# Slot offsets of the first layer's software pipeline in a two-layer decoder kernel

## The chip, the cores and the metric

The kernel runs on one core of one Trainium2 chip. The metric is the device time of one execution in microseconds (us). Five engines work side by side: PE (TensorE, matrix products; its weight loads are PEld), DVE (VectorE), ACT (ScalarE), POOL (GpSimd) and SP (SyncE, which here only issues DMAs). Each has its own instruction stream, executed in the order in which it was written. They are tied together by semaphores alone.

## The reference, cut to what matters

The program is a decoder of two layers. Each has a self-attention, a cross-attention against a context and a feed-forward part, each followed by a residual sum and a layer norm. The change touches the attentions of the first layer only. Per batch element (16 of them, 128 positions of 256 channels) they compute:

```
q, k, v = bitlinear(x, w_q), bitlinear(x, w_k), bitlinear(x, w_v)   # rows rounded to 8 bits, ternary weights
a = softmax(q k^T / 4, causal) v            # 16 heads; the sequence is seen as 256 tokens of 256
x1 = layernorm(x + bitlinear(a, w_o))
q = rope(wq x1 + bq); k = rope(wk c + bk); v = wv c + bv
x2 = layernorm(x1 + wo softmax(q k^T / sqrt(8), mask) v + bo)       # 16 heads of 8 channels
```

x2 goes to DRAM (`x_mid`), and its logits for the choice of experts are kept. Routing, the experts, the second layer and the retrieval part follow; the change does not touch them.

## The kernel before

`first_layer_attentions` (L529) is a software pipeline over the 16 batch elements. Time is cut into numbered slots. `Slots(20)` (L491) says that a new batch element starts every 20 slots: a step with offset `o` is written for batch element `b` into slot `20 b + o`. Each engine's program is one loop over the slots. In each slot it holds, in a fixed order, the steps whose offset fits. A slot is no barrier. It only sets the order of the instructions within each engine's stream, and an engine goes on as soon as its semaphores let it. I call `offset mod 20` the place of a step: in the steady part of the pipeline all steps with the same place stand in the same slot, for different batch elements. So offset -25 and offset 95 both have place 15.

Two lanes of small pieces fill the slots (`Lane`, L508). The **query lane** computes scores with queries as rows: 4 own (self-attention) pieces and 16 cross pieces per batch element. Of each, DVE takes the row maxima straight from the PSUM bank (`reduce_maxima`, L443, rows L447 and L449). There are two such banks, so PE may write piece i only when DVE has reduced piece i-2 (`pe.wait_ge(reduced, i - 1)`, L695). The maxima are split in two bf16 parts (`own_two`, `cross_two`), turned by PE (L379), copied by ACT and laid by DMA as two more rows into the operand stack (`own_rows`, `cross_rows`, `lay_maxima` L345, DMA rows L350 and L352). The **key lane** then computes the scores again with keys as rows and the maxima subtracted by those rows; ACT takes their exponential (L892), and every fourth piece PE weighs the values with them (`own_values`, `cross_values`, L422 and L438). Both lanes hold 20 pieces in 20 slots, so each has a piece in every slot of the steady part.

The other steps of a batch element, by engine:

- DVE: `row_scales_of` (L473 to L480 and L1032), `round_rows_of` (L486, L488), `copy_v` (L1043), `own_heads` (L1072, L1074), `head_scales`, `round_heads`, `own_sum` with its moments (L1088, L464 to L468), `own_end` (L1095), `rotate` (L1101, L1102; for q and for k), `cross_recips` (L1109), `cross_heads` (L1113), `cross_sum` with its moments (L1117), `cross_end` (L1125), `keep_logits`. In a slot the reduction of the query piece comes first, then these.
- POOL: `root` (L1011), and `split_self` and `split_cross` (L336 to L342), which split an operand into three bf16 parts.
- SP: loads of x (L610) and of the context (L615), the DMAs that lay the parts into the stacks (`stack_part` L355, `stack_side` L367), the store of x2 (L631). SP waits in order: what is written behind a waiting DMA waits too.
- PE: the small products and transposes between these. They share the PSUM bank `work` (query, key and value products), the bank `bank_a` (own values, heads, output product) and a small bank (maxima, sums, output, logits), and wait on the semaphores of whoever read the bank last. `make_cross_v` (L792), for one, waits until DVE has rotated k (`k_rotated`).

DMA rows are named by their issuing queue: SPq, ACTq.

Of the kernel before, what the change touches and what calls it, by code (L numbers as in the profile page):

```python
# [528 lines left out]
def first_layer_attentions(nc, d, t, ps):  # L529

    ctx = ExitStack()
    with ctx:
# [53 lines left out]
        block = ctx.enter_context(nc.Block())  # L586

        slots = Slots(20)
        OWN_SCORES, CROSS_SCORES, OWN_KEYS, CROSS_KEYS = 0, ((39, 1), (44, 15)), 9, ((65, 4), (73, 12))
        LOAD_ROWS, ROW_SCALES, ROUND_ROWS, TURN_ROWS, COPY_ROWS, MAKE_QK, SCALE_QK, MAKE_V, COPY_V, TURN_QK, COPY_QK = -33, -25, -24, -18, -18, -16, -16, -14, -13, -12, -12  # L590
        SPLIT_SELF, STACK_FIRST, STACK_SECOND, STACK_THIRD = -8, -7, -6, -5
        OWN_TWO, TURN_OWN_MAXIMA, OWN_ROWS, OWN_VALUES, COPY_OUT, TURN_OUT, OWN_HEADS, HEAD_SCALES, ROUND_HEADS = 3, 5, 5, 14, 15, 17, 18, 19, 20
        TURN_HEADS, COPY_HEADS, MAKE_O, OWN_SUM, ROOT_A, OWN_END = 22, 22, 24, 25, 25, 27
        LOAD_CONTEXT, MAKE_CROSS_K, ROTATE_K, SPLIT_KEYS, STACK_KEYS = 5, 11, 12, 15, 25
        MAKE_CROSS_Q, ROTATE_Q, SPLIT_QUERIES, STACK_QUERIES = 29, 29, 30, 31
        MAKE_CROSS_V, COPY_CROSS_V, CROSS_TWO, TURN_CROSS_MAXIMA, CROSS_ROWS = 53, 53, 58, 60, 60
        CROSS_VALUES = (70, 78, 82, 86)
        COPY_CROSS_OUT, CROSS_RECIPS, LAY_RECIPS, SPREAD_SUMS, CROSS_HEADS, MAKE_Y, CROSS_SUM, ROOT_X, CROSS_END = 87, 89, 90, 92, 92, 94, 95, 96, 98
        STORE_ROWS, TURN_X2, COPY_X2, MAKE_LOGITS, KEEP_LOGITS = 99, 101, 101, 103, 104
        query_lane = slots.lane(OWN_SCORES, CROSS_SCORES, SELF0.banks, CROSS0.banks)  # L600
        key_lane = slots.lane(OWN_KEYS, CROSS_KEYS, SELF0.banks, CROSS0.banks)
        SLOTS = range(LOAD_ROWS, slots.window * (B - 1) + KEEP_LOGITS + 1)
# [51 lines left out]
        def _(pe):  # L654
# [140 lines left out]
            def cross_values(b, g):  # L795
                i = key_lane.index("cross", b, GROUP * g)
                if g == 0:
                    pe.wait_ge(xv_copied, 2 * b + 2)
                    if b >= 1:
                        pe.wait_ge(out_x_copied, b)  # L800
                pe.wait_ge(probs_made, i + GROUP)
                weigh_shared(pe, out_x, [probs[(i + j) % RING] for j in range(GROUP)], t["v_cross0"][b % 2], GROUP * g).then_inc(probs_used, 1)
# [31 lines left out]
            for s in SLOTS:  # L834
# [16 lines left out]
                for g in range(4):  # L851
                    if (b := slots.batch_at(s, CROSS_VALUES[g])) is not None:
                        cross_values(b, g)
# [685 lines left out]
def second_layer_attentions(nc, d, t, ps):  # L1539

    ctx = ExitStack()
    with ctx:
# [140 lines left out]
        def _(pe):  # L1683
# [85 lines left out]
            def own_values(b):  # L1769
                i = key_lane.index("own", b, 0)  # L1770
                if b >= 1:
                    pe.wait_ge(sum_a_made, b)
                pe.wait_ge(v_copied, b + 1)
                pe.wait_ge(probs_made, i + GROUP)
                weigh_values(pe, SELF1, bank_a, [probs[(i + n) % RING] for n in range(GROUP)], t["v_self1"][b % 3], 0).then_inc(probs_used, 1)
# [19 lines left out]
            def cross_values(b, n):  # L1795
                i = key_lane.index("cross", b, n)
                if n == 0 and b >= 1:
                    pe.wait_ge(sum_x_made, b)
                if n == 0:
                    pe.wait_ge(xv_copied, b + 1)  # L1800
                pe.wait_ge(probs_made, i + GROUP)
                weigh_values(pe, CROSS1, out_x, [probs[(i + j) % RING] for j in range(GROUP)], t["v_cross1"][b % 2], n).then_inc(probs_used, 1)
# [27 lines left out]
            for s in SLOTS:  # L1830
# [14 lines left out]
                if (b := slots.batch_at(s, OWN_VALUES)) is not None:  # L1845
                    own_values(b)
                if (b := slots.batch_at(s, CROSS_VALUES)) is not None:
                    cross_values(b, 0)
# [723 lines left out]
def program(nc, d, out):  # L2572

    ctx = ExitStack()
    with ctx:
# [25 lines left out]
        with ExitStack() as stage:  # L2601
            sb, _ = open_tensors(nc, stage, "kept")
            for att, n in ((SELF0, 2), (CROSS0, 3)):
                t[f"stack_{att.name}"] = [sb(f"stack_{att.name}_{u}", [att.rows + 2] + ([att.groups, 2 * D] if att.causal else [2, att.groups, D]), BF16) for u in range(n)]
            t["v_self0"] = [sb(f"v_self0_{u}", [P, HEADS, 32]) for u in range(2)]
            t["v_cross0"] = [sb(f"v_cross0_{u}", [P, 2 * XG // SHARED, 2, GROUP, 32]) for u in range(2)]
            prepare_weights(nc, d, t, ps)
            first_layer_attentions(nc, d, t, ps)
# [39 lines left out]
```

## Time and profile before

| | us |
|---|---|
| median of 3 runs | 1780.8 |
| lowest, highest run | 1767.7, 1783.01 |
| the profiled execution | 1767.65 |
| its span in the trace | 1765.9 |
| PE busy, share of the span | 1422.5, 81% |
| DVE busy | 975.9, 55% |
| ACT busy | 614.0, 35% |
| POOL busy | 418.3, 24% |

```profile
PE   2466888888888986399999993568888875899997
DVE  5456666666666652522222223367878752567775
PEclk9878999999999998599999996789999997899999
```

Each digit is the busy share of one fortieth of the span (44.1 us) in tenths; PEclk is the clock that TensorE was granted, in tenths of 2.4 GHz. The first layer's attentions lie in slices 2 to 16: their first score product starts at 60.60 us, the last logits are kept at about 711 us. Busy times are not a bound by themselves: what matters is which wait ends last in each stretch.

### The profile page before, as it was taken

Reading aid. Unit: us, or ns where it says so; the run is one execution under the profiler, and the core shown is the slowest. Engines: PE = TensorE matmul, PEld = TensorE weight load, DVE = VectorE, ACT = ScalarE, POOL = GpSimd, SP = SyncE. Lnnn points to the kernel's source line nnn. Section 1 sums busy time; section 2 is a strip of 40 time slices with the busy share of each in tenths; the row PEclk is TensorE's granted clock in tenths of the full one; section 3 lists DMA queues with packets and bytes.
Section 4 is the critical chain, followed back from the end, with each engine's and each line's share of the span. In section 5 each row is a group of like instructions: output and inputs, shape, how many; then the busy total and the mean of one; then the engine's idle time right before and its main releaser. Section 6 shows DMA issues by size and latency. Waiting matters only on the chain. (4 is left out here: it accounts for less than half of the span.)

```text
span 1765.9 us, 29494 instructions
## 1 busy us (share of the span) xinstructions
PE 1422.5 (81%) x9331; PEld 878.0 (50%) x9331; DVE 975.9 (55%) x2623; ACT 614.0 (35%) x1389; POOL 418.3 (24%) x588
## 2 busy tenths in 40 slices
PE   2466888888888986399999993568888875899997
PEld 1234555555555553155656562345555543566554
DVE  5456666666666652522222223367878752567775
ACT  0122444434444443022222231335555542232231
POOL 2233223322223200111111103454555420000000
PEclk9878999999999998599999996789999997899999
DMA  3245344533444310651111102664555420200000
GB/s 89 58 50 66 47 60 53 64 51 54 54 53 56 45 24 9 233 180 68 32 35 34 33 25 55 172 119 103 113 110 118 98 51 20 72 1 13 12 1 25
DMA packets 165337, 112.77 MB, mean 64 GB/s; under 512 B 32690, under 2 KB 155826, under 8 KB 165056
## 3 DMA queue, kind: packets, MB, share of 16 engines
q1 hardware_dynamic: 150272, 99.04, 27.7%
q0 software_dynamic: 3408, 9.31, 2.2%
q10 hardware_dynamic: 11504, 2.53, 0.8%
q8 instruction: 78, 1.28, 0.3%
q14 instruction: 75, 0.61, 0.1%
HBM read 46.48 MB, written 12.45 MB: 33 GB/s over the span
## 5 line engine op out<-in xcount | busy, mean ns | idle before, releaser
L892 ACT ACTIVATE first_probs<-pair 128x512 f32<-128x512 f32 x320 | 190.3, 597 | 302.6 <-PE pair L408 273.4
L449 DVE TENSOR_REDUCE first_negmax_x<-bank 128x2 f32<-128x512 f32 x256 | 177.0, 692 | 109.5 <-PE bank L393 96.1
L1885 ACT ACTIVATE second_probs<-pair 128x512 f32<-128x512 f32 x192 | 113.8, 598 | 129.2 <-PE pair L408 112.6
L393 PE MATMUL bank<-kept_stack_cross 96*128 96x256 bf16 x768 | 150.4, 277 | 9.7 <-DMA kept_stack_cross<-second_parts_x_q 7.9
L408 PE MATMUL pair<-kept_stack_cross 98*128 98x256 bf16 x768 | 148.8, 276 | 1.5 <-DMA kept_stack_cross<-second_rows_x 1.0
L1439 PE MATMUL pair<-kept_w,experts_hidden_t 128*128 x312 | 141.5, 596 | 0.0
L386 PE MATMUL bank<-kept_mask_q,kept_ident 128*128 128x512 bf16 x256 | 99.3, 388 | 35.0 <-DVE first_negmax_x L449 26.8
L449 DVE TENSOR_REDUCE second_negmax_x<-bank 128x2 f32<-128x512 f32 x128 | 88.5, 692 | 60.2 <-PE bank L393 52.2
L393 PEld LDWEIGHTS bank<-kept_stack_cross 96*128 96x128 bf16 x768 | 74.1, 101 | 74.3 <-issue 21.2
L1480 ACT ACTIVATE experts_hidden_t<-bank,kept_b 128x128 f32<-128x128 f32 x156 | 44.4, 367 | 187.4 <-PE bank L1414 187.4
L1394 POOL DMA_INDIRECT experts_expert_rows<-x_mid,kept_row_of x39 | 36.9, 947 | 276.4 <-PE bank L1406 250.3
L401 PE MATMUL pair<-kept_mask_t,kept_ident 128*128 128x512 bf16 x256 | 98.4, 384 | 2.5 <-ACT first_probs L892 1.5
L1439 PEld LDWEIGHTS pair<-kept_w,experts_hidden_t 128*128 128x128 f32 x312 | 60.0, 193 | 76.0 <-issue 76.0
L408 PEld LDWEIGHTS pair<-kept_stack_cross 98*128 98x128 bf16 x768 | 74.5, 100 | 41.5 <-issue 3.5
L386 PE MATMUL bank<-kept_causal_q,kept_ident 128*128 128x512 bf16 x128 | 53.5, 418 | 48.9 <-DMA kept_stack_self<-first_parts_a 24.6
L1517 DVE COPY experts_hidden<-pair 128x512 f32<-128x512 f32 x39 | 27.0, 691 | 108.7 <-PE pair L1439 108.7
L1430 PE MATMUL bank<-kept_w,experts_expert_rows_t 128*128 x156 | 77.9, 624 | 5.5 <-DMA kept_w<-in_L_ffn_W 4.1
L1448 PE MATMUL pair<-kept_w,experts_hidden_t 128*128 x312 | 73.9, 380 | 1.4 <-ACT experts_hidden_t L1488 1.4
L438 PE MATMUL pair<-first_probs,kept_v_cross 128*32 128x256 f32 x1024 | 68.5, 385 | 3.7 <-ACT first_probs L892 3.7
L401 PE MATMUL pair<-kept_causal_t,kept_ident 128*128 128x512 bf16 x128 | 53.0, 414 | 20.0 <-DMA kept_stack_self<-first_rows_a 19.2
L2442 POOL TENSOR_TENSOR retrieve_stats<-retrieve_stats,kept_minus_half 128x1 f32<-128x1 f32 x16 | 8.9, 557 | 251.3 <-DVE retrieve_stats L468 251.3
L1511 DVE COPY experts_hidden<-bank 128x512 f32<-128x512 f32 x39 | 27.0, 691 | 71.2 <-PE bank L1430 71.2
(430 smaller groups left out, 2974.1 us busy)
## 6 DMA issues: line engine op xcount, KB each, us to landing
kept_stack_self<-first_parts_a SPq DMA_DIRECT2D x128, 64.0 KB, 5.6
kept_w<-in_L_ffn_W SPq DMA_DIRECT2D x16, 512.0 KB, 7.5
kept_w<-in_L_ffn_W SPq DMA_DIRECT2D x8, 1024.0 KB, 7.0
kept_stack_self<-second_parts_a SPq DMA_DIRECT2D x128, 64.0 KB, 3.4
kept_stack_cross<-first_parts_x_k SPq DMA_DIRECT2D x96, 64.0 KB
kept_stack_cross<-first_parts_x_q SPq DMA_DIRECT2D x96, 64.0 KB
kept_stack_cross<-second_parts_x_k SPq DMA_DIRECT2D x96, 64.0 KB
kept_stack_cross<-second_parts_x_q SPq DMA_DIRECT2D x96, 64.0 KB
```

The lines of the kernel that those rows point to most:

```text
L386: pe.matmul(bank[:, :], ident16, mask, start=True, stop=False, skip_group_check=True)
L393: mm = pe.matmul(out, q, k, start=mask is None, stop=True, skip_group_check=True)
L401: pe.matmul(bank[:, :], ident16, mask, start=True, stop=False, skip_group_check=True)
L408: mm = pe.matmul(out, k, q, start=mask is None, stop=True, skip_group_check=True)
L438: mm = pe.matmul(out[j * 32:(j + 1) * 32, at * D:(at + 1) * D], values[:, 2 * k + at, a, j, :], probs[j][:, k * D:(k + 1) * D], start=(a = ...
L449: return dve.tensor_reduce(negmax[:, 2 * n:2 * n + 2], bank[:, :].rearrange("p (m t) -> p m t", t=D), AX.X, ALU.max, negate=True)
L892: act.activation(probs[i % RING][:, :], key_bank[i % 2][:, :], ACT.Exp, scale=att.scale).then_inc(probs_made, 1)
L1430: mm = pe.matmul(layer1_bank[:, :], rows_t[n % 2][:, k, :], t["w1"][:, bass.ds(expert, 1), k, :].rearrange("p a f -> p (a f)"), start=(k = ...
L1439: mm = pe.matmul(layer2_bank[:, :], hidden1_t[n % 2][:, k, :], t["w2"][:, bass.ds(expert, 1), k, :].rearrange("p a f -> p (a f)"), start=( ...
L1448: mm = pe.matmul(layer3_bank[:, 0:D], hidden2_t[n % 2][:, k, :], t["w3"][:, bass.ds(expert, 1), k, :].rearrange("p a f -> p (a f)"), start ...
L1480: ins = act.activation(hidden1_t[n % 2][:, k, :], turn1_bank[:, k * P:(k + 1) * P], ACT.Gelu, bias=t["b12"][:, k, bass.ds(expert, 1)])
L1885: act.activation(probs[i % RING][:, :], key_bank[i % 2][:, :], ACT.Exp, scale=att.scale).then_inc(probs_made, 1)
```

## The change

Only numbers move. No instruction is added or taken away, and the order inside a slot is the same. The last slot of the loop is 410 instead of 404, its first one -31 instead of -33.

```
-        OWN_SCORES, CROSS_SCORES, OWN_KEYS, CROSS_KEYS = 0, ((39, 1), (44, 15)), 9, ((65, 4), (73, 12))
-        LOAD_ROWS, ROW_SCALES, ROUND_ROWS, TURN_ROWS, COPY_ROWS, MAKE_QK, SCALE_QK, MAKE_V, COPY_V, TURN_QK, COPY_QK = -33, -25, -24, -18, -18, -16, -16, -14, -13, -12, -12
-        SPLIT_SELF, STACK_FIRST, STACK_SECOND, STACK_THIRD = -8, -7, -6, -5
-        OWN_TWO, TURN_OWN_MAXIMA, OWN_ROWS, OWN_VALUES, COPY_OUT, TURN_OUT, OWN_HEADS, HEAD_SCALES, ROUND_HEADS = 3, 5, 5, 14, 15, 17, 18, 19, 20
-        TURN_HEADS, COPY_HEADS, MAKE_O, OWN_SUM, ROOT_A, OWN_END = 22, 22, 24, 25, 25, 27
-        LOAD_CONTEXT, MAKE_CROSS_K, ROTATE_K, SPLIT_KEYS, STACK_KEYS = 5, 11, 12, 15, 25
-        MAKE_CROSS_Q, ROTATE_Q, SPLIT_QUERIES, STACK_QUERIES = 29, 29, 30, 31
-        MAKE_CROSS_V, COPY_CROSS_V, CROSS_TWO, TURN_CROSS_MAXIMA, CROSS_ROWS = 53, 53, 58, 60, 60
-        CROSS_VALUES = (70, 78, 82, 86)
-        COPY_CROSS_OUT, CROSS_RECIPS, LAY_RECIPS, SPREAD_SUMS, CROSS_HEADS, MAKE_Y, CROSS_SUM, ROOT_X, CROSS_END = 87, 89, 90, 92, 92, 94, 95, 96, 98
-        STORE_ROWS, TURN_X2, COPY_X2, MAKE_LOGITS, KEEP_LOGITS = 99, 101, 101, 103, 104
+        OWN_SCORES, CROSS_SCORES, OWN_KEYS, CROSS_KEYS = 0, ((44, 16),), 11, ((67, 4), (75, 12))
+        LOAD_ROWS, ROW_SCALES, ROUND_ROWS, TURN_ROWS, COPY_ROWS, MAKE_QK, SCALE_QK, MAKE_V, COPY_V, TURN_QK, COPY_QK = -31, -26, -24, -18, -18, -16, -16, -14, -13, -12, -12
+        SPLIT_SELF, STACK_FIRST, STACK_SECOND, STACK_THIRD = -10, -9, -8, -7
+        OWN_TWO, TURN_OWN_MAXIMA, OWN_ROWS, OWN_VALUES, COPY_OUT, TURN_OUT, OWN_HEADS, HEAD_SCALES, ROUND_HEADS = 3, 5, 5, 16, 17, 19, 21, 23, 24
+        TURN_HEADS, COPY_HEADS, MAKE_O, OWN_SUM, ROOT_A, OWN_END = 26, 26, 28, 29, 29, 31
+        LOAD_CONTEXT, MAKE_CROSS_K, ROTATE_K, SPLIT_KEYS, STACK_KEYS = 5, 14, 15, 16, 27
+        MAKE_CROSS_Q, ROTATE_Q, SPLIT_QUERIES, STACK_QUERIES = 33, 33, 34, 36
+        MAKE_CROSS_V, COPY_CROSS_V, CROSS_TWO, TURN_CROSS_MAXIMA, CROSS_ROWS = 57, 57, 59, 61, 61
+        CROSS_VALUES = (72, 80, 84, 88)
+        COPY_CROSS_OUT, CROSS_RECIPS, LAY_RECIPS, SPREAD_SUMS, CROSS_HEADS, MAKE_Y, CROSS_SUM, ROOT_X, CROSS_END = 89, 92, 93, 96, 97, 99, 100, 101, 105
+        STORE_ROWS, TURN_X2, COPY_X2, MAKE_LOGITS, KEEP_LOGITS = 106, 107, 107, 109, 110
```

A pair `(r, m)` of a lane stands for m pieces in slots r, r+1, and so on. Before, the first cross score of a batch element stood alone in slot 39, ahead of the next element's own scores. Now all 16 stand in slots 44 to 59.

## Rows read from the trace of the kernel before

**Rows 1.** Part 1 of the page: busy time of each engine, share, instructions

```profile
PE 1422.5 (81%) x9331; PEld 878.0 (50%) x9331; DVE 975.9 (55%) x2623; ACT 614.0 (35%) x1389; POOL 418.3 (24%) x588
```

**Rows 2.** Stretches: length, busy us per engine, granted clock, DMA share, GB/s

```profile
211.50:582.00 370.50, 315.52 (x2762) 194.92 (x2760) 244.47 (x596) 158.04 (x320) 111.24 (x160) 0.99 0.42 56
320.50:357.10 36.60, 31.12 (x279) 19.26 (x278) 24.40 (x61) 15.81 (x32) 11.13 (x16) 1.00 0.45 57
582.00:664.50 82.50, 72.42 (x602) 42.90 (x600) 52.41 (x114) 35.18 (x70) 11.97 (x20) 1.00 0.19 29
```

**Rows 3.** PE's waits, 211.5 to 582: total us, times, longest

```profile
PE bank L386 <- DVE first_negmax_x L449: 22.1, 20, 1.8
PE pair L401 <- DMA kept_stack_self<-first_rows_a: 14.1, 9, 1.7
PE bank L386 <- DVE first_negmax_a L447: 9.1, 10, 1.4
PE bank L792 <- issue: 7.4, 10, 0.7
```

**Rows 4.** Timeline 349.8 to 354.5: start, us, engine, line, operation, idle before

```profile
349.83 0.69 DVE L449 TENSOR_REDUCE first_negmax_x<-bank 128x2 f32<-128x512 f32 x1 [2.25 <-PE bank L393]
...
350.07 0.38 PE L386 MATMUL bank<-kept_mask_q,kept_ident 128*128 128x512 bf16 x1
...
350.44 0.48 DVE L1117 SCALAR_TENSOR_TENSOR first_sum_x<-pair,kept_bo,first_x 128x256 f32<-128x256 f32 x1
...
350.95 0.38 PE L386 MATMUL bank<-kept_mask_q,kept_ident 128*128 128x512 bf16 x1
...
351.88 0.42 DVE L473 TENSOR_REDUCE first_qs<-first_x 128x1 f32<-128x256 f32 x1
...
353.45 0.69 DVE L449 TENSOR_REDUCE first_negmax_x<-bank 128x2 f32<-128x512 f32 x1
354.06 0.34 DVE L486 TENSOR_SCALAR first_whole<-first_x,first_qs 128x256 f32<-128x256 f32 x1
...
354.20 0.39 PE L386 MATMUL bank<-kept_mask_q,kept_ident 128*128 128x512 bf16 x1 [1.77 <-DVE first_negmax_x L449]
```

**Rows 5.** Timeline 365 to 374: the maxima's rows and what waits for them

```profile
365.37 3.97 SPq L374 DMA_DIRECT2D kept_stack_cross<-first_parts_x_k  x6
...
367.73 1.33 ACTq L350 DMA_DIRECT2D kept_stack_self<-first_rows_a  x2
...
373.85 0.39 PE L401 MATMUL pair<-kept_causal_t,kept_ident 128*128 128x512 bf16 x1 [1.70 <-DMA kept_stack_self<-first_rows_a]
```

**Rows 6.** Timeline 383 to 385: the rotation of k and the value product

```profile
383.67 0.47 DVE L1102 SCALAR_TENSOR_TENSOR first_sind_k<-bank,kept_bqk_rot,kept_sin 128x256 f32<-128x256 f32 x1
...
384.25 0.68 PE L792 MATMUL bank<-kept_xw_t,first_kv 128*128 128x128 f32 x4 [0.74 <-issue]
```

**Rows 7.** A stretch of 3.4 us at the lower clock

```profile
374.30:377.70 3.40, 3.40 (x14) 2.18 (x12) 1.59 (x4) 0.60 (x1) 0.32 (x1) 0.50 0.00 0
```

**Rows 8.** PE's waits for stacked operands, 60.6 to 211.5

```profile
PE bank L386 <- DMA kept_stack_self<-first_parts_a: 24.6, 5, 10.6
PE bank L386 <- DMA kept_stack_cross<-first_parts_x_q: 8.1, 2, 6.7
```

**Rows 9.** Timeline 89 to 110: from the third element's operands to its scores

```profile
89.11 0.60 ACT L912 ACTIVATE first_full_a<-bank 128x512 f32<-128x512 f32 x1 [3.48 <-PE bank L685]
...
93.98 3.90 SPq L374 DMA_DIRECT2D kept_stack_cross<-first_parts_x_q  x6
...
96.09 1.05 POOL L336 TENSOR_TENSOR first_parts_a<-first_full_a,kept_ones_bf 128x512 bf16<-128x512 f32 x1
...
96.34 0.95 DVE L486 TENSOR_SCALAR first_whole<-first_x,first_qs 128x256 f32<-128x256 f32 x1
...
103.77 1.23 SPq L362 DMA_DIRECT2D kept_stack_self<-first_parts_a  x1
...
109.77 0.61 PE L386 MATMUL bank<-kept_causal_q,kept_ident 128*128 128x512 bf16 x1 [4.73 <-DMA kept_stack_self<-first_parts_a]
```

## The prediction

> **What bounds the kernel now.** I read the busy shares first. PE is busy 81% of the span, DVE 55% [rows 1], so the whole leans on PE, but the share says nothing of the stage that changes. So I cut the first layer into stretches. Between 211.5 and 582 us the pipeline is full: ten batch elements take 370.5 us, and PE is busy for 315.5 of them. One undisturbed element takes 36.6 us with 31.1 of PE work; DVE's is 24.4 and POOL's 11.1 [rows 2]. So about 5.4 us per element are PE idle. PE's work stays, and the question is only how much of that idle time the new places remove.
>
> PE's waits in the same stretch name it [rows 3]. DVE's maxima come late for 22.1 + 9.1 = 31.2 us, the DMA with the own maxima for 14.1, and the value product L792 stands 7.4 us with "issue" as its releaser. They make 52.7 us of the 55.0 that are idle.
>
> **Change, part 1: DVE's pile-up at places 15 and 16.** Before, place 15 holds the reduction, the cross sum with its moments and the row scales; place 16 adds the rounding. The timeline shows it [rows 4]: reduction at 349.83, cross sum at 350.44, row scales at 351.88, and the next reduction only at 353.45, that is 3.6 us for one slot of DVE. PE passes a bare slot in 350.95 - 350.07 = 0.88 us, fills both score banks and waits 1.77 us. This is the largest of the waits. After the change the cross sum has place 0, the row scales 14, the rounding 16. I lay out the whole window of 20 slots with the rows' prices: reduction 0.7 plus 0.6 from the start of a score piece until it can be reduced, a sum with moments 1.45 and row or head scales 1.5 [rows 4], a rotation 0.95 from two instructions of 0.47 [rows 6], 0.88 for PE's two pieces, and the rest of PE's 31.1 us laid on the slots where its steps now stand. The fullest slot of DVE becomes place 3 (reduction, own maxima, head scales: 2.6 us), and place 4 has 1.5 us of extra PE work to cover it. Two tight spots are left. At places 9 to 12 PE has two nearly bare slots, while DVE has the own sum: the piece of place 12 waits about 0.6 us. At places 13 and 14 the key product now follows the query product by one slot, and the bank is free only when DVE has rotated q: about 0.25 us. With small ones elsewhere that makes 1.1 us per element. The bounds are 0 (all is covered) and the present 3.1 per element. I take 1.5, nearer to the layout because its prices are rows of this trace, a little above it because it has no jitter.
>
> **Part 2: L792.** The value product needs k rotated. DVE ends that at 384.14 and PE starts at 384.25 [rows 6], so "issue" hides a wait on DVE, one slot behind the rotation. Now the rotation has place 15, the product 17, and behind the second stands 2 us of other PE work at place 16. The 7.4 us go; what could remain is inside the 1.5 above.
>
> **Part 3: own keys two slots later.** The maxima's rows are issued by ACT from 367.73 to 369.06 and released PE at 373.85 after 1.70 us of waiting [rows 5]. Transit is 4.8 us, behind six DMAs of SP (365.37 to 369.34) on the same engines. The turning stays at place 5, the keys go from 9 to 11. Places 9 and 10 are 1.25 and 0.88 us of PE, and values that used to be weighed at other places now fall on place 8. So PE arrives at least 2.1 us later, against 1.7 that it was late. The 14.1 us go. If they went on being late by their difference it would be a few tenths; if the transit doubled, all of it would stay. SP's six key DMAs move from place 5 to 7, so they start slightly behind the rows instead of ahead; that helps rather than hurts.
>
> Sum for the steady stretch: 52.7 removed, 15 put back, so **-38**.
>
> **Part 4: the clock.** At 374.30, right behind that wait, TensorE's clock falls from 2.4 to 1.2 GHz for 3.4 us [rows 7], and PE is busy all through it, so it costs about half, 1.7 us. The stretch's mean is 0.99 [rows 2], 1% of 370.5 us off full speed, which is 3.7 us of the lower level's half and so about three such falls. Where PE does not wait, they have no cause that I can see. I take **-4**; between 0 and -5. The Trainium skill says the same (TensorE: Matmul & The Clock Gate, Part 1: activity releases the throttle); by it all three would go.
>
> **Part 5: filling the pipeline.** Up to 211.5 us PE waits for stacked operands, 24.6 and 8.1 us [rows 8]. The first wait, 10.6 us, is the first element's latency and stays. For the third element see the timeline [rows 9]: its operands are ready at 89.7, but POOL splits them only at 96.09, since the first element's query split stands before it, and SP has six query DMAs in front (93.98 to 97.88). The last part is issued at 103.77 and PE starts at 109.77. Now the own split (place 10) stands ahead of the query split (14). It starts near 90.5, because the root at place 9 still precedes it; SP needs about 6.5 us for its ten DMAs, then 6 us of transit: near 104, 6 us earlier. Besides the 10.6 and the 4.7 at 109.77, 9.3 us of such waits are left; I lay nearly all on the two elements that follow, for the same reason. Against this, cross scores start 5 slots later for the first element. I take **-15**, between -5 (half of each wait comes back as another) and -21.
>
> **Part 6: draining.** From 582 to 664.5 PE is idle for 10.1 of 82.5 us [rows 2]; of this I count 5 as the same waits. But more work is left behind slot 300: one score piece, two key pieces and about a fifth of the other steps of one element, 3 us. Net **-2**, between +3 and -5. The last chain of the stage, value sums to logits, keeps its steps, and an empty slot costs nothing.
>
> What moves without a price: the load of x (place 7 to 9) stands 5 slots ahead of its use instead of 8; rival C. The store of x2 and the logits move by 6 to 7 slots, nothing waits for them inside the stage. The reciprocals get 3 slots after the copy, not 2. The x1, key-stack and probability buffers keep their distances.
>
> **Sum.** -38 - 4 - 15 - 2 = -59. The profiled execution took 1767.65, so its like takes 1708.6. The median shown is 13 us above that execution, the lowest run equals it; I add half of the distance and predict **1714 us**.
>
> **A rule that speaks against it.** The split on POOL now runs beside other DVE steps. While POOL works on L336 (96.09 to 97.14), DVE's L486 takes 0.95 us [rows 9] instead of 0.34 [rows 4]. The Trainium skill says why (SBUF, State Buffer, "Who interferes with whom"): DVE and GpSimd share a pair of ports, and one holds it for a whole instruction. In the new order `own_end` at place 11 falls beside the own split and the rounding at 16 beside the key split. Three instructions held by 0.6 to 1 us each make up to 2.2 us of DVE per element. In the layout DVE runs ahead at both places, so I price it at nothing; without that cover it is rival B.
>
> **The rivals.**
> A. DVE's waits do not go, they move: places 9 to 15 hold the own sum, both rotations and the row scales. For: these are 5 of DVE's longest steps within 7 slots, and PE's slots there are short. Against: none shares a slot with another. Then 31.2 + 7.4 stay and the steady part brings 14: -14 - 15 - 2 = -31, 1743 with the same half distance.
> B. The shared ports: 2.2 us for each of some 14 elements give back 31 of 59: -28, 1746. For: the row at 96.34. Against: DVE is idle for a third of the element [rows 2].
> C. **Slower**: SP's queue. The load of x has place 9, and it waits for the own sum of three elements earlier, which now has place 9 as well. It is issued some 2 us into place 9 and the row scales need it about 9.4 us into it. Transit is at most the 6 us of the stacks, so there is 1 us of slack. It decides from a transit of 13 us on: then DVE stands 4.5 us per element, all that parts 1 to 3 bring; at 16 us it would cost 3 us times 14, +25 on balance, 1799. Against: SP's other DMAs at that time are few.
> D. No change worth measuring: the saved waits come back as waits on operands, as PE reaches each DMA's landing sooner. 1774.
>
> **Chances.** Forecast 0.70, A 0.12, B 0.06, D 0.07, C 0.05. A measurement of this kernel can tell about 1% (18 us) from no change. Faster by over 1%: forecast, A and B, 0.88; within 1%: D, 0.07; slower: C, 0.05. The range starts at 1690, where nearly all idle time and all of part 5 go (-80 on the lowest run), and goes up to 1750, which takes in A and B. Left out are D, C and the tails of the forecast, 0.2 in all.
>
> **What would show it.** Right: elements in the full stretch take 32 to 33 us instead of 36.6; DVE's waits before L386 fall below 1.5 us per element; no wait of L401 on the own rows; L792 without its 0.74; own scores of the third element near 104 us; PEclk 1.00 from about 180 to 560 us. Wrong: a wait of DVE's L473 for x (C), L1095 or L486 near 1 us together with waits of PE (B), or PE's waits gathered before the pieces of places 12 to 15 (A).

## The result, and the profile after

The changed kernel takes 1688.6 us (median of 4 runs, 1686.03 to 1690.56) where the kernel before took 1774.25 in the same comparison: a ratio of 0.9515, 95% interval 0.9482 to 0.9549. That is 86 us less. I forecast 60 less, with 1690 as the lower end, so the direction was right and the size too small. The profiled execution took 1686.03, its span is 1684.2; 81.7 us of span are gone.

Parts 1 and 2 of the page after (busy time; tenths in 40 slices of 42.1 us):

```profile
PE 1400.9 (83%) x9221; PEld 874.6 (52%) x9331; DVE 982.0 (58%) x2623; ACT 609.2 (36%) x1389; POOL 419.8 (25%) x588
...
PE   2478999999999954899999946588888875999997
...
PEclk9679999999999976999999976799999996999999
```

Counted from 1, PE is at 9 in slices 5 to 14, where it stood at 8 in all but one. This trace lacks 110 of PE's 9331 matmul records (x9221), so its PE busy times are a little low and the idle rows of PE are bounds.

Stretches of both kernels, cut where the 1st, 3rd, 6th and 16th element's own scores begin, then at the end of the scores and of the stage (columns: stretch, length, busy of PE, PEld, DVE, ACT, POOL, clock, DMA share, GB/s). After:

```profile
60.50:99.70 39.20, 24.77 (x188) 15.33 (x190) 19.28 (x51) 10.54 (x21) 16.00 (x22) 0.76 0.30 63
99.70:188.60 88.90, 75.14 (x605) 47.69 (x617) 68.09 (x157) 32.15 (x67) 33.48 (x48) 0.89 0.42 68
188.60:505.10 316.50, 302.24 (x2712) 191.69 (x2761) 248.42 (x593) 152.60 (x320) 112.16 (x160) 1.00 0.38 65
505.10:583.60 78.50, 72.84 (x612) 43.48 (x623) 53.90 (x117) 34.62 (x70) 11.94 (x20) 1.00 0.22 31
583.60:626.80 43.20, 28.72 (x216) 14.83 (x217) 8.63 (x25) 15.81 (x31) 1.65 (x3) 0.85 0.04 12
626.80:1684.20 1057.40, 884.71 (x4837) 553.98 (x4868) 554.25 (x1568) 360.33 (x876) 228.69 (x320) 0.92 0.28 72
```

And the same of before, where [rows 2] do not hold it:

```profile
60.60:109.80 49.20, 26.52 (x194) 16.21 (x195) 21.90 (x60) 10.18 (x21) 17.60 (x24) 0.77 0.42 62
109.80:211.30 101.50, 80.30 (x637) 49.17 (x638) 66.68 (x152) 32.69 (x68) 32.29 (x46) 0.89 0.47 54
...
664.50:710.50 46.00, 30.84 (x215) 15.27 (x215) 8.02 (x22) 15.25 (x29) 1.09 (x2) 0.80 0.04 11
710.50:1765.90 1055.40, 882.88 (x4868) 551.23 (x4868) 552.59 (x1568) 359.55 (x876) 228.20 (x320) 0.92 0.28 72
```

Filling (to the 6th element's scores) went from 150.7 to 128.1 us, -22.6. The full stretch of ten elements went from 370.6 to 316.5, -54.1, so an element now takes 31.65. Draining went from 128.6 to 121.7, -6.9. All that follows: +2.0. The gain lies where it was forecast (-38 and -4 in the full stretch, -15 in filling, -2 in draining), and each stretch gained more than its terms.

The changed kernel was profiled once more in a later comparison (a0_changed). That trace has all 9331 matmul records, so its idle time of PE in the full stretch can be trusted: 316.90 - 306.04 = 10.9 us, where it was 55.0 before.

```profile
188.40:505.30 316.90, 306.04 (x2762) 191.80 (x2761) 248.12 (x593) 152.61 (x320) 111.97 (x160) 1.00 0.38 65
```

PE's waits in the full stretch, which answer to [rows 3]:

```profile
PE bank L386 <- DVE first_negmax_x L449: 4.4, 12, 0.4
PE bank L773 <- issue: 3.7, 6, 0.9
...
PE bank L386 <- DVE first_negmax_a L447: 0.5, 1, 0.5
```

31.2 us for DVE's maxima have become 4.9. L401's wait for the rows and L792's for the rotation are gone. The key product L773 waits now, as the layout by hand had it for places 13 and 14: 0.37 us per element, where it had 0.25. The waits named by these rows are 8.6 us (9.0 in a0_changed) where I had put back 15.

The third element's operands, timeline after, to be read beside [rows 9]:

```profile
88.59 0.60 ACT L912 ACTIVATE first_full_a<-bank 128x512 f32<-128x512 f32 x1 [1.87 <-PE bank L685]
...
89.54 1.05 POOL L336 TENSOR_TENSOR first_parts_a<-first_full_a,kept_ones_bf 128x512 bf16<-128x512 f32 x1
...
97.35 0.60 SPq L362 DMA_DIRECT2D kept_stack_self<-first_parts_a  x1
...
99.75 0.10 PEld L386 LDWEIGHTS bank<-kept_causal_q,kept_ident 128*128 128x128 bf16 x1 [3.22 <-DMA kept_stack_self<-first_parts_a]
...
100.15 0.63 PE L393 MATMUL bank<-kept_stack_self 96*128 96x128 bf16 x4 [3.39 <-DMA kept_stack_self<-first_parts_a]
```

The split starts 6.6 us earlier and the last part is issued 6.4 us earlier. PE goes on at 99.75, where the weights for the first own score are loaded (the record of its product is one of those missing). That is 2.4 us after the last issue, not 6.0: the transit fell to less than half as well. In a0_changed, whose records are complete, it is 2.5.

### The profile page after: what moved, and what is told of

The parts are those of the page before. It is cut to its first block and busy times, and to the rows that moved or that the text cites. A ratio compares the mean times of both kernels' runs of the same rounds, so it can differ in the third digit from the quotient of the medians.

```text
span 1684.2 us, 29387 instructions
## 1 busy us (share of the span) xinstructions
PE 1400.9 (83%) x9221; PEld 874.6 (52%) x9331; DVE 982.0 (58%) x2623; ACT 609.2 (36%) x1389; POOL 419.8 (25%) x588
## 5 line engine op out<-in xcount | busy, mean ns | idle before, releaser
L1885 ACT ACTIVATE second_probs<-pair 128x512 f32<-128x512 f32 x192 | 113.7, 598 | 130.8 <-PE pair L408 111.6
L1480 ACT ACTIVATE experts_hidden_t<-bank,kept_b 128x128 f32<-128x128 f32 x156 | 44.6, 368 | 186.4 <-PE bank L1414 186.4
L386 PE MATMUL bank<-kept_mask_q,kept_ident 128*128 128x512 bf16 x221 | 86.4, 391 | 20.4 <-DVE first_negmax_x L449 11.8
L401 PE MATMUL pair<-kept_mask_t,kept_ident 128*128 128x512 bf16 x249 | 94.7, 380 | 1.8 <-ACT first_probs L892 1.8
L1488 ACT ACTIVATE experts_hidden_t<-bank,kept_b 128x128 f32<-128x128 f32 x156 | 44.7, 368 | 50.3 <-PE bank L1422 50.3
L2315 PE MATMUL pair<-retrieve_x_t,kept_gate_w 128*128 128x512 f32 x128 | 61.9, 607 | 0.0
```

The source lines that it names most:

```text
L386: pe.matmul(bank[:, :], ident16, mask, start=True, stop=False, skip_group_check=True)
L401: pe.matmul(bank[:, :], ident16, mask, start=True, stop=False, skip_group_check=True)
L1885: act.activation(probs[i % RING][:, :], key_bank[i % 2][:, :], ACT.Exp, scale=att.scale).then_inc(probs_made, 1)
L2315: mm = pe.matmul(bank[:, :], t[weights][:, j, u * P:(u + 1) * P], x5_t[g % 2][:, j, :], start=(j == 0), stop=(j == KT - 1))
```

## The experiments

Offsets of the same code, changed in the kernel before (b...) or in the changed one (a..., c...). The table has the time, its ratio to the kernel before in the same comparison, and from one profile of each the filling, the full stretch (ten elements) and the draining. The draining ends here with the last logits, a few tenths of a us before the ends taken above. An effect on the time is told against the kernel that the run started from: the one before in the same comparison for b..., a0_changed (1687.2) for a... and c1_key_product, which were timed in other comparisons than a0_changed.

| kernel | median us | ratio, 95% interval | filling | full | draining |
|---|---|---|---|---|---|
| before | 1773 to 1776 | 1 | 150.7 | 370.6 | 128.0 |
| b1_scales | 1756.95 | 0.9905 (0.9878 to 0.9931) | 150.9 | 356.1 | 128.0 |
| b2_value | 1762.97 | 0.9935 (0.9907 to 0.9963) | 150.0 | 362.8 | 127.7 |
| b3_keys | 1832.47 | 1.0326 (1.0281 to 1.0372) | 162.2 | 412.3 | 134.1 |
| b4_split | 1768.14 | 0.9952 (0.9928 to 0.9975) | 146.0 | 371.1 | 131.8 |
| b5_row | 1772.55 | 0.9987 (0.9973 to 1.0001) | 150.4 | 368.5 | 130.8 |
| b7_split_row | 1769.05 | 0.997 (0.9949 to 0.9991) | 145.3 | 370.5 | 128.7 |
| b8_split_scales | 1757.08 | 0.9911 (0.9878 to 0.9943) | 146.0 | 356.0 | 129.9 |
| b10_queue | 1762.16 | 0.9921 (0.989 to 0.9952) | 136.4 | 368.5 | 130.7 |
| b6_all | 1800.1 | 1.0144 (1.0117 to 1.0172) | 145.2 | 396.1 | 134.5 |
| b9_sums | 1736.68 | 0.9792 (0.973 to 0.9855) | 137.6 | 346.4 | 122.6 |
| a0_changed | 1687.2 | 0.9513 (0.9485 to 0.9541) | 127.2 | 316.9 | 121.3 |
| a1_pile | 1727.64 | 0.9733 (0.9691 to 0.9775) | 134.1 | 345.2 | 121.3 |
| a2_rows | 1696.77 | 0.9572 (0.9538 to 0.9607) | 130.1 | 317.9 | 123.0 |
| a3_split | 1819.0 | 1.0253 (1.0212 to 1.0293) | 163.3 | 408.9 | 122.8 |
| a4_recips | 1703.72 | 0.9592 (0.9547 to 0.9636) | 127.6 | 327.7 | 123.5 |
| c1_key_product | 1681.07 | 0.9488 (0.9449 to 0.9527) | 127.3 | 312.0 | 120.3 |
| c1_again | 1681.06 | 0.9477 (0.9454 to 0.95) | 126.9 | 310.5 | 121.2 |

### One part at a time, in the kernel before

**b1_scales**

```
- ROW_SCALES = -25
+ ROW_SCALES = -26
```

> The kernel before, with the row scales alone moved from place 15 to 14, so that they no longer share a slot with the cross sum. Theory 1 (waits are independent and each is worth its row in PE's waits): the 1.76 us before the piece of place 17 go in each of some 14 elements, -25 us, an element of 36.6 us becomes 34.8. Theory 2 (a removed wait gives more than PE's row, since PE's idle row starts only when the modelled end of the last product is over; the weight-load row of the same wait, 2.0 to 2.1 us, is the price): -29 us. Theory 3 (waits replace one another: DVE is late anyway two slots on): the waits of places 0 and 1 grow, -10 us or less.

Its waits in the full stretch:

```profile
PE pair L401 <- DMA kept_stack_self<-first_rows_a: 14.7, 10, 1.7
PE bank L386 <- DMA kept_stack_self<-first_parts_a: 7.7, 9, 1.3
PE bank L792 <- issue: 7.4, 10, 0.7
PE bank L386 <- DVE first_negmax_a L447: 5.2, 10, 0.9
PE bank L386 <- DVE first_negmax_x L449: 3.6, 11, 0.3
```

DVE's 31.2 us fell to 8.8, so the pile-up at place 15 caused 22.4 us of them, but only 14.5 us came back: 7.7 of the 22.4 turned into a wait for the own operands, which had been just in time. By the medians it is -19 us, between theory 1 (-25) and theory 3 (-10 or less).

**b2_value**: `MAKE_CROSS_V, COPY_CROSS_V = 54, 54` for 53, 53.

> The kernel before, with the value product and its copy alone moved from place 13 to 14, two slots behind the rotation of k instead of one. Theory 1 (PE's row): 0.74 us per element, -10 us. Theory 2 (weight-load row, 1.0 us): -14 us. Theory 3 (the wait was covering for DVE's later ones, which grow by the same): within 4 us of before.

L792's wait is gone, so "issue" hid the rotation. By the medians it is -13 us, between theories 1 and 2. The full stretch is 7.8 us shorter, but that this is L792's 7.4 us is luck:

```profile
211.00:573.90 362.90, 319.89 (x2761) 197.18 (x2762) 244.93 (x595) 157.88 (x320) 111.03 (x160) 0.97 0.44 57
```

PE is idle for 43.0 us instead of 55.0, 12 less, since DVE's waits fell too (31.2 to 24.6), with 3.1 us of new waits for the own operands. And PE is busy 4.4 us longer, at a clock of 0.97 instead of 0.99: the clock fell to its lower level seven times instead of three, each time within 1.5 us behind a wait of PE of 1.6 to 1.8 us.

**b3_keys**

```
- OWN_KEYS, CROSS_KEYS, CROSS_VALUES = 9, ((65, 4), (73, 12)), (70, 78, 82, 86)
- MAKE_CROSS_Q, ROTATE_Q, SPLIT_QUERIES, STACK_QUERIES, ROW_SCALES = 29, 29, 30, 31, -25
+ OWN_KEYS, CROSS_KEYS, CROSS_VALUES = 11, ((67, 4), (75, 12)), (72, 80, 84, 88)
+ MAKE_CROSS_Q, ROTATE_Q, SPLIT_QUERIES, STACK_QUERIES, ROW_SCALES = 31, 31, 32, 33, -23
...  (what follows from the keys: + 2)
```

> The kernel before, with the key lane and all that follows from it two slots later, and the row scales moved along with the cross sum (both now place 17), so that DVE's pile stays as it was and only the distance from the own maxima's rows to the own keys grows, 4 slots to 6. Theory 1: the wait of L401 on the rows goes, 1.6 us in each of some 12 elements, -19 us, and DVE's wait before L386 stays near 3 us per element. Theory 2 (weight-load rows, 2.0 us, and the falls of the clock behind that wait go too): -24 to -30 us. Theory 3: the transit follows the keys, the wait stays, 0.

All three were wrong on the time: 57 us slower. L401's wait for the rows went, and so did DVE's 31.2 us (0.2 are left). In their place PE waits 40.7 us for the own operands, 15.6 before the key product L773 and 8.8 for the cross queries. Query split and own split now share place 12, the queries first. Timeline of this kernel:

```profile
334.86 1.04 POOL L336 TENSOR_TENSOR first_parts_a<-first_full_a,kept_ones_bf 128x512 bf16<-128x512 f32 x1
...
342.57 0.60 SPq L362 DMA_DIRECT2D kept_stack_self<-first_parts_a  x1
...
348.56 0.61 PE L386 MATMUL bank<-kept_causal_q,kept_ident 128*128 128x512 bf16 x1 [4.21 <-DMA kept_stack_self<-first_parts_a]
```

Its full stretch, 41.7 us longer than before, shows the loss in two parts:

```profile
222.60:634.90 412.30, 339.17 (x2760) 205.66 (x2760) 242.64 (x592) 156.62 (x320) 110.90 (x160) 0.91 0.37 50
```

PE is idle for 73.1 us, 18 more, and busy for 24 more on the same products, with a granted clock of 0.91 instead of 0.99. Its waits are longer now (up to 4.4 us), and more than half of what this stretch lost is PE's own busy time.

**b4_split**

```
- SPLIT_SELF, STACK_FIRST, STACK_SECOND, STACK_THIRD = -8, -7, -6, -5
+ SPLIT_SELF, STACK_FIRST, STACK_SECOND, STACK_THIRD = -11, -10, -9, -8
```

> The kernel before, with the own split on POOL alone moved ahead of the query split (place 12 to 9, its DMAs to 10, 11 and 12). My account of the filling: the third element's own scores start 6 us or more earlier (before 109.77 us), the two after it gain too, -10 to -20 us in all, nothing in the steady stretch (36.6 us per element stay). Rival (the cross scores of slot 39 wait in front of the own scores in PE's order, and their operands are now later by the own split): the gain in the filling is 3 us or less, or a loss.

Nearer to the rival: the third element's own scores start at 108.7, 1.0 us earlier. The filling is 4.7 us shorter, and the time 7 us by the medians.

**b5_row**: `CROSS_SCORES = ((44, 16),)` and `CROSS_TWO = 59`.

> The kernel before, with the cross scores alone in one row (slots 44 to 59, own maxima of the cross lane at 59), so that no cross score stands ahead of the next element's own scores. Theory: alone it does little, since the own scores wait for their own operands at that place anyway: 0 to -5 us, the filling 2 us shorter at most, 36.6 us per full element. Rival: the lone piece at slot 39 is what holds the filling back (it waited 6.7 us in the kernel before): -8 us or more.

As the theory says: -3 us by the medians, and the interval of the ratio reaches 1, so the row alone is not measurable.

### Two and more parts together

**b7_split_row**: b4 and b5.

> The kernel before with two parts of the change: own split ahead of the query split, and the cross scores in one row. The split alone brought 1 us at the third element (108.7 against 109.8) because the cross score of slot 39, whose operands were then later, stood in front of the own scores. Theory (the two only pay together): third element's own scores near 100 us as in the changed kernel, filling 15 to 20 us shorter, -15 to -20 us in all. If the parts simply add: -7 us and what the row brings alone.

Not so. The third element's own scores start at 107.8, and the two together bring -7 us by the medians, no more than the split alone. The timeline shows what was in front now (SP's issues, then PE):

```profile
93.24 0.60 SPq L364 DMA_DIRECT2D kept_stack_self<-first_parts_a  x1
...
95.48 4.70 SPq L374 DMA_DIRECT2D kept_stack_cross<-first_parts_x_q  x6
...
102.77 0.60 SPq L362 DMA_DIRECT2D kept_stack_self<-first_parts_a  x1
...
107.83 0.61 PE L386 MATMUL bank<-kept_causal_q,kept_ident 128*128 128x512 bf16 x1 [10.44 <-DMA kept_stack_self<-first_parts_a]
```

POOL had the own parts ready, but in SP's stream the queries (slot 31) stand before the own parts two and three (31 and 32).

**b10_queue**: b7 with `STACK_QUERIES = 33` for 31.

> The kernel before with own split first, cross scores in one row, and SP's query DMAs at 33 instead of 31, behind the own ones. Without the last, SP issued six query DMAs between the own parts (95.5 to 100.2) and the third element's own scores began at 107.8. Theory (the filling is set by the order of SP's queue as much as by POOL's): they begin near 101 to 103, the first five elements end 12 to 18 us earlier than in the kernel before, -12 to -18 us in all. Rival (PE or DVE is the limit there once the split is early): within 3 us of the variant without it, -5 in all.

```profile
97.14 0.60 SPq L362 DMA_DIRECT2D kept_stack_self<-first_parts_a  x1
97.79 4.28 SPq L374 DMA_DIRECT2D kept_stack_cross<-first_parts_x_q  x6
...
100.23 0.39 PE L386 MATMUL bank<-kept_causal_q,kept_ident 128*128 128x512 bf16 x1 [1.51 <-DMA kept_stack_self<-first_parts_a]
```

The theory holds: 100.2, the filling is 14.3 us shorter and the time 13 us by the medians. With none of SP's query DMAs in between or right ahead, 3.1 us pass from the last issue to PE's start (2.4 in the changed kernel), instead of 5.1 in b7 and 6.0 before. The counterpart is b6 below, where six key DMAs of SP stand right ahead of the own ones: 6.4 us, and its third element starts at 104.4.

**b8_split_scales**: b1 and b4.

> The kernel before with two parts: row scales out of the pile-up (place 14) and own split ahead of the query split. With the row scales alone PE began to wait for the own operands, 7.7 us in the full stretch. Theory (the own operands were late as soon as PE was faster, and the split's place covers that): the full stretch falls from 356 to about 347 us, -28 us in all. If the operands' wait was an accident of one run: 356 us, -24.

The wait for operands went, but DVE's is at 18.3 us instead of b1's 8.8, and the full stretch is unchanged at 356.0. PE ran on into the next late reduction. I was wrong to expect more.

**b6_all**: b3's key lane, b4, b5 and b1 (`ROW_SCALES = -26`, `ROUND_ROWS = -24`).

> The kernel before with all parts at once in their plain form: keys and what follows two slots later, own split at place 9, row scales at 14, cross scores in one row; nothing spread further. The key lane's move alone cost 57 us, because the query split moved with it and pushed the own split. Theory (that loss was the own operands' alone): with the own split in front it turns round, -60 to -80 us, close to the changed kernel. Rival (the finer spreading of DVE's steps in the changed kernel is worth most): -40 us or less.

24 us slower than before, against theory and rival. The timeline names a chain (ACT's DMA of the sums, SP's own parts behind it, then DVE, ACT and PE):

```profile
381.11 0.67 ACTq L954 DMA_DIRECT2D first_sums<-first_heads_x  x1
381.72 0.59 SPq L360 DMA_DIRECT2D kept_stack_self<-first_parts_a  x1
...
388.03 0.35 DVE L1109 RECIPROCAL first_recips<-first_sums 128x32 f32<-128x32 f32 x1 [5.41 <-DMA first_sums<-first_heads_x]
...
389.10 0.60 ACT L892 ACTIVATE first_probs<-pair 128x512 f32<-128x512 f32 x1 [5.00 <-DVE first_recips L1109]
...
389.18 1.19 PE L773 MATMUL bank<-first_kv,kept_xw_t 128*128 128x256 f32 x2 [3.72 <-issue]
```

L773 waits for DVE's rotation of q, which stands behind the reciprocals in DVE's stream (31.5 us in ten elements). But the sum of PE's waits hardly grew:

```profile
205.70:601.70 396.00, 337.56 (x2760) 206.33 (x2761) 253.87 (x593) 156.73 (x320) 112.06 (x160) 0.91 0.36 52
```

PE is idle for 58.4 us, 3.4 more than before. The other 22 of the 25.5 us that this stretch is longer are PE's own busy time, at a clock of 0.91: few long waits (up to 3.9 us) cost more than many short ones (up to 1.8 us) of the same sum.

**b9_sums**: b6 with `CROSS_RECIPS, LAY_RECIPS, SPREAD_SUMS, CROSS_HEADS, MAKE_Y, CROSS_SUM, ...` and the cross maxima (61) as in the change.

> The plain form of all parts (25 us slower than the kernel before) with one thing more: the chain of the cross sums laid out as in the changed kernel, from the reciprocals at 92 to the logits at 110. Theory (the plain form loses by this chain alone): the wait of DVE for the sums falls from 5 us to under 2, PE's 3.2 us before the key product L773 go, an element takes 33 us instead of 39.6, 50 to 90 us less than the plain form. Rival (the own DMAs at places 10 to 12 sit behind the sums in the queue wherever the reciprocal stands): under 25 us less.

63 us faster than b6 by the medians, within the theory's range: moving the chain of the sums takes the loss away. Not as the theory had it, though. The sums arrive as late as in b6, up to 7.3 us after their issue, and DVE still waits 29.4 us for them in ten elements (48.3 in b6). What went is PE's wait before L773, and with it the lower clock:

```profile
198.40:544.80 346.40, 311.14 (x2762) 194.72 (x2761) 254.73 (x593) 156.05 (x320) 111.74 (x160) 0.99 0.43 60
```

Of the 49.7 us that this stretch is shorter than b6's, 23 are idle time and 26 are busy time. b9 moves fifteen offsets at once, the cross sum and the last norm among them. Which of them counts is not shown, save for the reciprocals (a4). The full stretch is still 30 us longer than the changed kernel's, and PE waits 25.0 us for DVE's maxima there (13.1 + 11.9) and 5.5 at L792, against 4.9 and 0. So the places of the other steps are worth about 30 us more. No run moves them one by one.

### Parts taken back, in the changed kernel

**a1_pile**: `ROW_SCALES, ROUND_ROWS = -20, -19`, so the scales share place 0 with the cross sum.

> The changed kernel, with the row scales put back into one slot with the cross sum (both place 0) and the rounding right behind them (place 1), all else as changed. If DVE's pile-up is what part 1 says, PE waits 1.7 to 2.1 us per element again before a piece near place 2, +25 to +30 us against the changed kernel. If the even spread matters little because PE's longer slots (values at place 0) cover it, under +8 us.

+28.3 us in the full stretch and +40 by the medians, more than expected. The wait is another one than I named, not the banks but the transpose behind the rounding:

```profile
PE bank L667 <- DVE first_xq L488: 24.8, 10, 2.8
```

The wait for the banks stays at 4.1 us. The rounding had stood six slots ahead of its transpose in both kernels, and here it stands one slot ahead. So the run prices that distance, and it is no proof for the pile-up before the banks; b1 alone is.

**a2_rows**: `TURN_OWN_MAXIMA, OWN_ROWS = 7, 7`; `TURN_X2, COPY_X2, MAKE_LOGITS, KEEP_LOGITS = 108, 108, 110, 111`.

> The changed kernel, with the turning of the own maxima and their rows at place 7 instead of 5 (and the logits' steps one slot later, which share the bank), so 4 slots lie between rows and keys as before. By part 3 the wait of L401 comes back in most elements: the transit of 4.8 us stands against places 8 to 10, now 2.5 + 1.2 + 0.9 us. If the distance in slots decides, +1.5 us per element, about +20. If what decides is PE's work in these slots, and the weighing of values now at place 8 is enough cover, less than +5.

```profile
PE pair L401 <- DMA kept_stack_self<-first_rows_a: 1.2, 7, 0.2
```

The full stretch grew by 1 us, so four slots are enough in the new order. PE's work in them is not what covers the rows: PE reaches L401 4.0 to 4.1 us after the start of the last rows' issue, where it was 3.7 in the kernel before. The rows themselves come earlier, 4.2 us after that start instead of 5.0 to 5.4. Of the six key DMAs of SP, three are issued ahead of them now, and five before. That this is the reason is likely, but no run shows it. The 9.6 us of the medians are only partly seen in this profile (filling +2.9, draining +1.7).

**a3_split**: `SPLIT_SELF, STACK_FIRST, STACK_SECOND, STACK_THIRD = -5, -4, -3, -2`.

> The changed kernel, with the own split on POOL and its DMAs behind the query split again (place 15, DMAs 16, 17 and 18). By my account of the filling the loss is there alone: the third element's own scores 6 to 10 us later (now 99.7), +10 to +22 us in all. Rival (the split's order matters in the steady stretch as well, since only 2 slots lie between the last DMA and the scores): elements of 31.6 us grow by a us or more, +25 or worse.

```profile
PE bank L386 <- DMA kept_stack_self<-first_parts_a: 78.4, 10, 8.1
```

The rival, and far beyond it: 132 us slower than the changed kernel, 92 of them in the full stretch.

```profile
224.30:633.20 408.90, 324.30 (x2760) 195.33 (x2760) 255.05 (x592) 152.61 (x320) 111.30 (x160) 0.92 0.41 50
```

74 of the 92 are more idle time of PE, 18 are more busy time at a clock of 0.92. It was the dearest distance of all that were tried, but the split stands three places later here than even in the kernel before.

**a4_recips**: `CROSS_RECIPS, LAY_RECIPS = 91, 92`.

> The changed kernel with the reciprocals of the cross sums and their laying one slot earlier (91 and 92), so 2 slots lie between the copy whose DMA brings the sums and the reciprocal, as before, instead of 3. I priced this distance at nothing. Theory: in the plain form of all parts DVE stood 5 us per element for these sums, with ACT and PE behind it, so the distance matters: DVE waits 1 to 2 us more per element at place 11, PE 0.5 to 1.5 us, +7 to +20 us against the changed kernel. Rival (only the place of the own DMAs behind the sums' matters): under +5.

+16.5 us by the medians, 10.8 in the full stretch, as the theory has it. One slot less for the sums, and DVE waits up to 3.1 us for them; behind it the query product L782 waits 9.9 us for x1.

### Further

**c1_key_product**: `MAKE_CROSS_K, ROTATE_K, SPLIT_KEYS = 10, 11, 15`, and **a0_changed**, **c1_again** beside each other.

> A try to go further: the changed kernel with the cross key product at place 10 instead of 14, its rotation at 11 instead of 15, its split at 15. The product then fills a nearly bare slot of PE behind DVE's own sum, and is no longer one slot behind the query product. If the waits left in the changed kernel are these two (before L386 near place 12, and before L773), 0.5 to 1 us per element less: -7 to -14 us against the changed kernel. If DVE's total is what counts there, no difference.

> The changed kernel itself, unedited, to compare with the next one on the same chip: 0.951 of the kernel before.

> The changed kernel with the key product at place 10 (L773), its rotation at 11 and split at 15, timed beside the changed kernel. If the 4.5 us that its full stretch was shorter in one profile are real, it is 4 to 10 us below the changed kernel, with little overlap of their runs; if not, no difference.

The first comparison had no changed kernel in it. The second gave 1681.06 (1676.03 to 1684.38) beside 1687.2 (1682.1 to 1695.92): 6 us less, where I had expected 7 to 14 at first and then 4 to 10, with an overlap of 2 us only. The full stretch is 310.5 beside 316.9, and no wait before L773 is left. Against the kernel before the ratio is 0.9477 (0.9454 to 0.95), and the changed kernel's is 0.9513 (0.9485 to 0.9541): these intervals still overlap, so a gain of 6 us over the changed kernel is likely and small.

## Why the prediction was wrong

The direction and the waits that go were right, and the sizes of several terms were too small. The two steps that failed most are the 15 us put back for waits that stay, of which 8.6 were there, and the 6 us of transit in the filling, of which 2.4 were there. The forecast of 1714 is 25.4 us above the 1688.6 measured. In the terms of the sum: the full stretch gave 54.1 instead of 42 (12.1 more), filling 22.6 instead of 15 (7.6 more), draining 6.9 instead of 2 (4.9 more), the rest of the program took back 2.0 that I had not counted, and the step from profiled run to median was 2.6 instead of 5.4 (2.8 more).

**Part 1, DVE's pile-up.** The cause was right: b1 takes away 22.4 of the 31.2 us by one offset. The step that failed is what was put back, 15 us for the waits that stay. The rows show 8.6 in ten elements, 0.9 each. The layout by hand had given 1.1, which is 2.4 us too much in ten elements, and raising it to 1.5 "for jitter" added another 4. Waits outside the four rows (2.3 us of L685 and L782), to which I gave nothing, went too.

**Part 2, L792.** Right (b2): its wait goes with one more slot.

**Part 3, own keys.** The wait went, 14.1 us, and PE does come later, as forecast: 6.1 us after the start of the last rows' issue instead of 3.7. But the two slots more were not needed for it. In a2 four slots do, since the rows come about 1 us earlier in the new order. And the key lane's move alone loses 57 us (b3), which the prediction did not foresee.

**Part 4, the clock.** The clock fell three times in the full stretch before, at 374, 449 and 562 us, each time right behind a wait of L401 of 1.7 us, and never in the changed kernel's (1.00). Three times half of 3.4 us are 5.1, I took 4. My working for "about three" does not come out: 3.7 us at 1.7 each are two, and the 0.99 it starts from is rounded. Less waiting alone does not do it, though: in b2 PE waited 12 us less, and the clock fell seven times. In the changed kernel, a2, a4 and c1, where PE's longest waits in the full stretch are 0.8 to 1.6 us, it never fell.

**The rest of the full stretch.** a0_changed has complete records: its full stretch is 53.7 us shorter than before, of which 44.1 are idle time and 5.1 the clock. The last 4.5 us lie in PE's busy time outside the falls of the clock; their cause stays open.

**Part 5, the filling.** -22.6 instead of -15. The third element's own scores come 10.0 us earlier instead of 6. The failed term is the transit: I carried 6 us over from [rows 9], but those DMAs of own parts stood behind six others of SP. With own parts first in SP's stream they need 2.4 to 3.1 us (changed kernel, b10). I had seen SP's queue as a delay of the issue alone. And POOL's order by itself brings 5 us; the order of SP's stream brings 9 more (b4, b7, b10). The rest of the filling gained 12.6 us where I had laid 9. It has a share of parts 2 and 3 as well, which I counted for the full stretch only: there L792 waited 1.8 us and L401 1.7 for the own rows before, and 0.2 and 0 in a0_changed.

**Part 6, draining.** -6.9 instead of -2. I counted half of the idle time as removable, and nothing in the last 46 us, which lost 2.8. No experiment was made for it. In the table the draining is 120 to 124 us wherever the chain of the sums has its new places (b9 and all a... and c...), and 128 to 135 in every other kernel. So the gain goes with that chain, of which I had said that it keeps its steps and that an empty slot costs nothing. Why it is shorter is not shown.

**What "moves without a price".** Here the argument was wrong, though it did no harm to the sum. The reciprocals' third slot is worth 16 us (a4), and the own split five places later costs over 100 (a3), though I priced its place in the filling alone. One by one the parts bring -19 (b1), -13 (b2), +57 (b3), -7 (b4) and -3 us (b5) by the medians. All but b2's together in plain form make +24, with the new chain of the sums -39, and as changed -86. So the parts do not add, and that the sum by parts came near is in part luck.

**Rivals.** A: of the 38.6 us that it let stay, 4.9 are left. B: DVE is held beside POOL. The rounding, which now runs beside POOL's key split, takes 0.65 us where it took 0.29 before:

```profile
L488 DVE TENSOR_SCALAR first_xq<-first_whole x9: 651/653/656, 217.1 to 470.0; 128x256 bf16<-128x256 f32 x9
```

The trace agrees with the rule of the Trainium skill (SBUF — State Buffer, "Who interferes with whom"): POOL's L336 runs from 311.75 to 312.36, and DVE's L488, begun at 311.86, ends at 312.51. That is 0.36 us in each element, covered as assumed; L486 and L1095 kept their 0.34 and 0.40 us, so the 2.2 us per element of the rival did not appear. (Three times 0.6 to 1 us are 1.8 to 3, not "up to 2.2".) C: no wait for x appeared. D: no change was wrong for the whole, but its mechanism is real in single parts, where saved waits came back as waits for operands (7.7 us in b1, 3.1 in b2, 40.7 in b3). The 1714 itself has a slip: 1708.6 and half of 13 are 1715.

## What to carry to other kernels

In a pipeline held together by orders, a wait of PE shows only the latest of several chains that are nearly as late. Before a wait is booked as gain, look up by how much the next chain is early (operands by split, queue and transit; sums; rows), and price every distance that the change lengthens as if it were missing. A transit read beside other DMAs is not the DMA's own: read what the issuing queues put right ahead of it and behind it. And look at the length of each wait, not at the sum alone: in b6 the sum hardly grew, and the lower clock behind the long ones cost 22 us.

## What the runs showed of the hardware

- Transit of the third element's last own part (64 KB), from the start of its issue to PE's start: 2.4 us in the changed kernel and 3.1 in b10, where the queries' DMAs stand behind the own ones; 5.1 in b7, where six of them stand between the own ones; 6.0 before and 6.4 in b6, where six other stack DMAs of SP stand right ahead of the own ones.
- The DMA of the sums (16 KB, ACT's queue), from the start of its issue to the reciprocal that waits for it, in the full stretch: 3.2 to 3.8 us before, with three key DMAs of SP issued in the 4 us ahead of it and none behind; 4.6 to 5.4 in b3 with six ahead and none behind; 6.6 to 7.1 in b6 with six ahead and seven to ten own ones behind. So DMAs ahead on the other queue delay it, and it came later still where many were issued behind it.
- Granted clock in the full stretch, beside PE's longest wait there: 1.00 in the changed kernel (0.9 us), 0.99 before (1.8), 0.91 in b3 (4.4) and b6 (3.9), 0.92 in a3 (8.1). Each fall is to half of 2.4 GHz.
- A DVE instruction of 0.29 us (L488) took 0.65 beside POOL's split, and in b6 L1095 took 0.94 us beside the own split instead of 0.40.
